# ScalarE's copy of an attention output bank out of PSUM: whole ahead of a step's exponentials, or in two halves around the first of them

## What is computed

```python
q = _apply_rope(q, cos, sin) * scale
k = _apply_rope(k, cos, sin)
attn = jnp.einsum('bhsd,bhtd->bhst', q, k)
attn = jax.nn.softmax(attn, axis=-1)
out = jnp.einsum('bhst,bhtd->bhsd', attn, v)
```

## Time and profile before

| | |
|---|---|
| median of 3 runs | 3391.24 us (3387.09 to 3391.94) |
| profiled execution, its own time | 3391.38 us |
| its span, first to last instruction | 3389.6 us |
| PE matmul busy | 96% of the span |
| VectorE busy | 88% |
| ScalarE busy | 74% |
| GpSimd busy | 64% |
| DMA engines, mean busy | 43% |

### The profile page before, as it was taken

How to read it: one execution, slowest core, us unless ns; L and a number is a source line. 1 busy time by engine, 2 the same in 40 slices (tenths; PEclk the granted TensorE clock), 3 DMA queues, 4 the chain that set the end, 5 groups by cost and what they waited for, 6 DMA issues and landing times.

```text
span 3389.6 us, 81479 instructions
## 1 busy us (share of the span) xinstructions
PE 3269.2 (96%) x30726; PEld 1787.8 (53%) x30726; DVE 2987.5 (88%) x5682; ACT 2512.9 (74%) x4884; POOL 2166.3 (64%) x2479
## 2 busy tenths in 40 slices
PE   6999999999999999999999999999999999999975
PEld 4434555555555555555555555555555555544444
DVE  7898999999999999999999999999999999989911
ACT  2777777777777777777777777777777777777730
POOL 3535766766776676677667667666766766644446
PEclk7999999999999999999999999999999999999977
DMA  6444455445445435544544453554455345334110
GB/s 200 114 97 96 96 113 107 99 109 113 100 98 114 104 93 115 116 97 99 116 102 94 113 119 92 104 115 98 98 113 111 94 110 113 95 78 76 38 40 26
DMA packets 312456, 341.19 MB, mean 101 GB/s; under 512 B 77184, under 2 KB 260352, under 8 KB 312064
## 3 DMA queue, kind: packets, MB, share of 16 engines
q1 hardware_dynamic: 312064, 335.99, 43.2%
HBM read 195.37 MB, written 140.51 MB: 99 GB/s over the span
## 4 chain that ended last, share of the span: by engine, by line
PE 94%; POOL 2%; DVE 2%; ACT 1%; DMA 1%; issue 1%; SPq 0%; POOLq 0%; DVEq 0%
PE ob L728 30%; PE sc L711 29%; PE job L583 25%; PE ms L700 9%; ACT prob L834 1%; DVE mxp L964 1%; POOL hid_r L1213 1%; PE ms L583 0%; PE job L636 0%; SPq L413 0%; PE ob L583 0%; PE sc L583 0%; POOL ka L1305 0%; DVE mxp L1104 0%; DVE hid L1012 0%
## 5 line engine op out<-in xcount | busy, mean ns | idle before, releaser
L964 DVE TENSOR_REDUCE mxp<-ms 128x1 f32<-128x512 f32 x4064 | 2619.0, 682 | 239.2 <-PE ms L700 193.2
L834 ACT ACTIVATE prob<-sc 128x512 f32<-128x512 f32 x4096 | 2225.1, 597 | 690.7 <-PE sc L711 665.8
L711 PE MATMUL sc<-qa,ka 50*128 50x512 f32 x4096 | 1547.9, 444 | 26.2 <-ACT prob L834 26.2
L700 PE MATMUL ms<-ka,qa 48*128 48x512 f32 x4064 | 1541.0, 445 | 4.0 <-DVE mxp L1104 2.2
L711 PEld LDWEIGHTS sc<-qa,ka 50*128 50x128 f32 x4096 | 684.6, 185 | 1120.1 <-ACT prob L834 964.2
L728 PE MATMUL ob<-prob,v_sb 128*17 128x512 f32 x8192 | 1082.3, 600 | 0.3
L700 PEld LDWEIGHTS ms<-ka,qa 48*128 48x128 f32 x4064 | 679.8, 185 | 12.2 <-DVE mxp L964 7.3
L1192 POOL TENSOR_TENSOR ve<-mv,eps_sb 128x2 f32<-128x2 f32 x128 | 24.9, 195 | 518.0 <-DVE mv L991 518.0
L1213 POOL TENSOR_TENSOR hid_r<-hid,hid_r 128x512 fp32r<-128x512 f32 x256 | 328.3, 1283 | 20.5
L583 PEld LDWEIGHTS job<-h_t,w_sb 64*128 64x128 f32 x3840 | 261.0, 186 | 23.4 <-issue 0.4
L728 PEld LDWEIGHTS ob<-prob,v_sb 128*17 128x17 f32 x8192 | 136.0, 95 | 257.5 <-issue 255.9
(11 more groups left out here) (145 smaller groups left out, 2820.9 us busy)
## 6 DMA issues: line engine op xcount, KB each, us to landing
qk_parts<-parts SPq DMA_DIRECT2D x124, 512.0 KB, 4.2
ka<-qk_parts SPq DMA_DIRECT2D x378, 128.0 KB, 4.6
qa<-qk_parts SPq DMA_DIRECT2D x378, 128.0 KB, 7.3
attention<-at_st SPq DMA_DIRECT2D x128, 256.0 KB, 3.7
v_ones<-v_st SPq DMA_DIRECT2D x64, 272.0 KB, 2.4
v_sb<-v_ones SPq DMA_DIRECT2D x64, 272.0 KB, 8.6
xn<-x SPq DMA_DIRECT2D x64, 256.0 KB, 4.8
ao<-attention SPq DMA_DIRECT2D x128, 128.0 KB
```

The costliest lines, as they stand in the source:

```text
L700: nc.tensor.matmul(ms[upto(b, g, NS1, at) % MS_BANKS][:, :], operand(qa, b, g, j, ROWS)[:, qt * P:(qt + 1) * P], operand(ka, b, g, j, ROWS ...
L711: nc.tensor.matmul(sc[upto(b, g, HG * STEPS, n) % SC_BANKS][:, :], operand(ka, b, g, j, ROWS + MROWS)[:, tt * P:(tt + 1) * P], operand(qa, ...
L834: nc.scalar.activation(prob[st_ % 2][:, j, :], sc[upto(b, g, HG * STEPS, n) % SC_BANKS][:, :], ACT.Exp).then_inc(s["exp_done"], 1)
L964: nc.vector.reduce_max(mxp[(b * G + g) % 2][:, kh, j * TT + qt:j * TT + qt + 1], ms[upto(b, g, NS1, at) % MS_BANKS][:, :], AX.X).then_inc( ...
```

## The change

ScalarE's copy is issued as two copies of 256 columns, each from the same bank to the same place as before. The first stands where the whole one stood, with its waits, ahead of the step's first exponential. The second stands between the first and the second exponential, has no wait of its own, and gives `o_taken`. Behind the last unit both stand together. The diff:

```diff
-            def take_outputs(b, g, qh):
-                act.wait_ge(s["pv_done"], upto(b, g, STEPS, (qh + 1) * TT))
-                wait_used(act, at_stored[qh], upto(b, g, 16, 0))
-                nc.scalar.activation(at_st[qh][:, :], ob[:, :], ACT.Copy).then_inc(s["o_taken"], 1)
+            def take_outputs(b, g, qh, side):
+                columns = slice(side * NQ // 2, (side + 1) * NQ // 2)
+                if side == 0:
+                    act.wait_ge(s["pv_done"], upto(b, g, STEPS, (qh + 1) * TT))
+                    wait_used(act, at_stored[qh], upto(b, g, 16, 0))
+                taken = nc.scalar.activation(at_st[qh][:, columns], ob[:, columns], ACT.Copy)
+                if side == 1:
+                    taken.then_inc(s["o_taken"], 1)
...
-                        if st_ == TT + 1:
-                            take_outputs(b, g, 0)
-                        if st_ == 1 and not (first and g == 0):
-                            take_outputs(b + (g - 1) // G, (g - 1) % G, 1)
-                        exps(b, g, st_, 0)
-                        exps(b, g, st_, 1)
+                        for side in range(2):
+                            if st_ == TT + 1:
+                                take_outputs(b, g, 0, side)
+                            if st_ == 1 and not (first and g == 0):
+                                take_outputs(b + (g - 1) // G, (g - 1) % G, 1, side)
+                            exps(b, g, st_, side)
...
-            take_outputs(B - 1, G - 1, 1)
+            for side in range(2):
+                take_outputs(B - 1, G - 1, 1, side)
```

## The result

| | before | changed |
|---|---|---|
| median | 3389.27 us (3387.09 to 3391.94, 4 runs) | 3419.81 us (3418.83 to 3430.08, 4 runs) |
| ratio | | 1.0097, 95% interval 1.0075 to 1.0118 |
| profiled execution: its time, span, mean TensorE clock | 3391.38, 3389.6, 0.980 | 3430.08, 3428.3, 0.974 |

The kernel is slower by 0.97%; 0.7% and 3415.8 us were forecast.

The account below looks back on a forecast made before the run. The second exponential's end, releasing the fourth scores load, was taken to pace the step. Terms of 22.1 (steps with a job), 2.2 (without) and 0.1 us (last copy) added 24.4 to 3391.4: 3415.8 us, range 3406 to 3424.

Parts of the forecast that it names:

- The bound: Step loop: first scores, two exponentials, fourth scores, `weigh`, next step; 3.08 us, with the second exponential releasing the fourth load.
- The first exponential back at 0.52 to 0.53: In a step with a copy, the shorter first piece lets this exponential start 0.10 to 0.12 us earlier than 0.64.
- The second piece at 1.02, the second exponential's end at 1.89: Times in us into a step 9; the exponential ended at 1.71 to 1.72 before the change.
- 0.18 a step, 123 x 0.18 = 22.1 us: Delay of the second exponential passing whole into each of 123 steps with a copy and a job.
- First pieces 0.18 further apart: Sign: starts of successive copies' first pieces 25.02 us apart instead of 24.84.
- The queues behind it: SP's DMA queue: store of `at_st` and later loads move 0.67 us; the reciprocal keeps over 2 us to spare.
- The four steps without a job, 2.2 us: Steps 1 and 9 of two batch 0 units: `weigh` waits for `o_taken`, 0.55 us later in each.
- The rule of the Trainium skill: ACTIVATE price: 186 ns plus 0.833 ns a column, neighbours overlapping by 93 ns; by it the total is 3414.2 us.
- No overlap: Rival: the piece between the exponentials overlaps neither neighbour, second exponential 0.40 us later, 3443 us; 5% given with halfway cases.
- absorbed: Rival: PE's work in a step has room to catch up; no change, 3391 give or take 5 us; 4%.
- the first exponential paces the step: Rival: PE waits for the third scores matmul, so 0.10 us a step comes back; 3379 us; 4%.
- The wait of PE's scores matmuls for exponentials: Sign: grows from 26.2 us, since PE runs out of work before the fourth scores matmul.

Follow-up runs that it names:

- e4: Changed kernel, but the four steps without a job keep the whole copy ahead of both exponentials; 3412.67 us, 1.0065 of the kernel before.
- e3: Changed kernel, but the whole 512-column copy between the exponentials in steps with a job, ahead of both in steps without; 3437.02 us, 1.0138 of before.
- e2: Changed kernel, but both halves ahead of the first exponential in steps with a job, whole copy ahead in steps without; 3395.78 us, 1.0019 of before.
- e8: Changed kernel, but 384 columns ahead and 128 between the exponentials, whole copy ahead in steps without a job; 3404.93 us, 1.0047 of before.
- e5_jobless_split: Changed kernel, but split only in the four steps without a job, whole copy ahead in all others; 3400.10 us, 1.0027 of the kernel before.
- e6: Changed kernel, but 384 columns ahead and 128 behind the second exponential, whole copy ahead in steps without a job; 3383.07 us, 0.9982 of before.
- e9: Changed kernel, but no split: whole copy behind the second exponential in step 1 with a job, ahead of the first elsewhere; 3393.02 us, 1.0011 of before.
- e10: As e6, but ScalarE's last job copy of step 9 takes 64 columns instead of 256, leaving results uncomputed; 3378.30 us, 0.9968 of the kernel before.
- e1: Changed kernel, but the second half behind the second exponential, whole copy ahead in steps without a job; 3387.14 us, 0.9997 of the kernel before.
- e7: As e1 in step 1 with a job only, whole copy ahead in step 9 and steps without a job; 3385.59 us, 0.9987 of before.

## Why the prediction was right

*The bound* was read rightly: four kernels that shift the second exponential's end by 0.18, 0.39, 0.06 and 0.07 us (e4, e3, e2, e8) lengthen the step by just that, and the batch by eight times that (1.43, 3.15, 0.46, 0.62).

*The first exponential back at 0.52 to 0.53*: 0.53 in the profile after. *The second piece at 1.02, the second exponential's end at 1.89*: 1.03 and 1.89. *0.18 a step, 123 x 0.18 = 22.1 us*: 3.36 against 3.18 and 3.19, and 22.0 us by e4_jobless_whole. *First pieces 0.18 further apart*: an eighth of a batch is 24.98 us, against 24.80. *Copies of 98.6 us in all*: 256 x 0.384 = 98.3.

*The queues behind it*: hidden, as said, though by less than the "over 2 us to spare". In steps with a job `weigh` starts 0.43 behind the fourth load as before. VectorE's reciprocals waited for the loads behind the store 5 times and 7.1 us, against 2 times and 3.7 us before. Three of the waits, of 0.4 us, are new and stand in the middle of the run, and the batches there are no longer for them.

*The four steps without a job, 2.2 us*, was mis-sized. The mechanism named there, a longer wait for `o_taken`, is in the trace (`weigh` 1.62 in, PE idle for 0.63 us until L842), and its own size was about right (0.55 us, once 0.36). But with these waits the granted clock is at its lower level for longer, and the four steps cost 9.2 us (5.4 to 12.9). No rival had the clock in it. I forecast 24.4 us more, and 0.97% is 32.9 (25.4 to 40.0), so the increase was forecast too small; this term is 7 of the 8.5 us between them. It also differs from run to run: the profiled execution, 10 us above the other three, has a mean clock of 0.974, they have 0.977 to 0.978.

*Luck in the total*: 3415.8 is only 4.0 us below the median, though the medians are 30.5 us apart and not 24.4, because the sum started at 3391.38, 2.1 us above the median of before.

*The rule of the Trainium skill* (ScalarE: Activation LUTs, What ACT_TABLE_LOAD costs) put one instruction more at 0.093 us of engine time; e2_both_ahead puts it at 0.05 to 0.06. For a piece of 128 columns an estimate by it is 0.293 us, the row has 0.27.

*No overlap*, *absorbed*, *the first exponential paces the step*: none occurred. The steps behind a late one take 3.09, and both intervals around the second piece, 1725.89 - 1725.39 = 0.50 and 1726.15 - 1725.89 = 0.26, are those of overlapped instructions. The wait of PE's scores matmuls for exponentials, which I expected to grow from 26.2 us, did not (25.9): in the trace of after PE's third matmul for the maxima, which runs beside the scores, lasts from 1726.38 to 1726.77, and the fourth scores matmul starts at 1726.81. The view merges the two scores matmuls into one row of 0.93 us, and a gap of 0.04 doesn't count as a wait. In e3_whole_between, where the delay is twice as long, the same wait is 62.3 us. For a delay of 0.18 that sign was badly chosen.

## What to carry to other kernels

An engine at 74% can pace one at 96%: lay one step's timeline beside the next and find the load that names its releaser. Splitting an instruction helps only if the part that is moved leaves the path; between the first and second of two instructions that a step waits for, it costs all the time that it holds the engine, 0.26 us here, of which only 0.10 came back ahead of them. Moving a piece off the path gains up to the next bound, and there were two within 0.1 us here, the word that a bank is free and the next job's operand. Try the piece sizes that fit between them.

## What was not expected of the hardware

The granted TensorE clock was at its lower level for longer when PE had four waits that were longer by 0.3 to 0.55 us: the three stretches of the changed kernel have 0.58, 0.51 and 0.54. By the timed runs of e5_jobless_split the price was more than four times the waits' length (9.2 us for 2.0), with an interval of 5.4 to 12.9 and single runs between 2 and 15 us above before.

Which waits set off which fall is shown in part. A fall right behind the waits of 0.63 us, at 185 us in the changed kernel and at 274 and 270 in it and in e5, is in no trace of a kernel that keeps the copy whole there; yet e5 has the wait of 0.63 at 183 us too, and no fall behind it. And a fall that begins at 225 to 229 us is also in seven of those (e2, e3, e4, e6, e8, e9, e10), for 7 to 20 us, and not in those of before, e1 and e7; in the changed kernel and e5 it lasts 24. Between 184 and 305 us the clock is 1.00 in before, e1 and e7, but 0.97 in e2 and e6, 0.96 in e4, 0.94 in e3, 0.93 in e9 and 0.92 in e8 and e10. So a fall of some hundredths there is no sign that the copy was split, while the only two traces with it split have 0.82 and 0.76. Which of the small falls come from the edits and which from chance, single traces don't tell.

The Trainium skill (TensorE: Matmul & The Clock Gate, A second HAM failure mode: psum-queue depth-cycling) tells of a kernel whose frequent short idle spells made the clock go back and forth between its levels. These traces agree in so far as the falls stand among steps in which PE idles for 0.45 us each, some with a wait of 0.63 or 1.24 us more; but before, the same steps with 0.45 and 1.24 and without the 0.63 show no fall.

The last units have low spells too, in the trace of before as well, and they move the time: the last batch, up to its last step, takes 199.2 us before, but 204.0 in the changed kernel and 193.8 in e5. A comparison of two single traces has that in it, which the medians of several runs and the length of the batches 2 to 13 have less or not at all.
